# Two graph layers on one core: all matmuls of the attention layer as pairs of 64 rows, with another order of the steps

## The chip, the cores and the metric

The kernel runs on one core of a Trainium2 chip, in one launch. The metric is the time of one execution on the device, in microseconds. A core has TensorE (PE: matrix products, with PEld for its weight loads), VectorE (DVE), ScalarE (ACT), GpSimd (POOL) and SyncE (SP), which issues the DMAs here. Each engine runs its own queue in order and waits on semaphores.

## What is computed

The input `x` is 32 batches of 512 x 512, `adj` a sparse weighted 512 x 512 graph.

```python
def layer0(x, adj, weight, bias):
    y = jnp.einsum('nm,bmd->bnd', adj, x)
    out = jnp.einsum('bnd,do->bno', y, weight) + bias
    return layernorm(x + out)

def layer1(x, w_qkv, w_proj, b_proj, ln_gamma, ln_beta, attn_mask):   # 8 heads of 64
    q, k, v = (x @ w_qkv) split in heads
    attn = softmax(where(attn_mask == 0, -inf, q k^T / 8))
    o = (attn v) @ w_proj + b_proj
    ln = layernorm(o) * ln_gamma + ln_beta
    return layernorm(x + o + ln)
```

All in float32. The kernel keeps that accuracy with three products: each operand is split into a part rounded to the reduced float32 format (`_hi`) and the rest (`_lo`), and hi x hi, hi x lo and lo x hi are summed in a PSUM bank. So each product leaves PSUM in two operations: ScalarE copies it rounded (`_hi`), VectorE subtracts that from the bank (`_lo`).

## The kernel before

The first stage does layer 0 batch by batch and stores its result, normalised and turned, in DRAM (lines up to 531). The change does not touch it. The second stage does layer 1. Its unit is a step: `k` counts 16 of them in a batch, 4 pairs of heads by 4 tiles of 128 query rows. Four steps with one pair of heads are a group, and the place of a step in it is its part, 0 to 3. For each step the work is:

- `scores` (line 778): q k^T for 2 heads, 128 x 512 each. A head has 64 rows, so the two heads lie in the two halves of the array and go to two banks; six matmuls, which are three pairs. Step `k` uses one of two pairs of score banks, and TensorE issues the scores for two steps together in every second step, two and three steps ahead.
- `masked_max` (1032): VectorE adds the mask and finds the row maximum; `exponent` (932): ScalarE; `inverse` (1038): VectorE; `normalise` (708, 711): GpSimd multiplies by the inverse of the sum.
- `turn` (790): TensorE transposes the probabilities in 16 pieces of 64 rows; `pt_hi_part` (939) and `pt_lo_part` (1045) take them out of the banks.
- Once in a group, in part 3, `attend_v` (824) multiplies by v on all 128 rows: 16 matmuls into two banks, which `ot_halves` (957, 959), `ot_sum` (1063), `ot_hi_part` (965) and `ot_lo_part` (1067) take away.

Between the transposes of two steps TensorE does fill from other parts of the work, 48 matmuls of 128 rows in each group: v (`v_matmuls`, 857) in group 0, the projection of the batch before (`project`, 875) in group 1, q and k of the next batch (`qk_matmuls`, 841) in groups 2 and 3. `FILL = [20, 12, 16, 0]` spreads them over the parts. Fill and `attend_v` share the banks `g_bank`. The first batch has no projection to fill group 1, the last no next batch for groups 2 and 3. The rows of the projection are finished by VectorE, ScalarE and GpSimd at steps in the tables `O_STEP`, `Z_STEP` and `S_STEP`. `ready_to_turn` holds the waits for the probabilities and for `pt_lo` of the step before; it stands ahead of the last fill matmul. The order is written out by hand in each engine's `batch`; the loop runs over batches 1 to 30.

Of the kernel before, what the change touches and what calls it, by code (L numbers as in the profile page):

```python
# [24 lines left out]
ALU = mybir.AluOpType  # L25
# [6 lines left out]
def graph_layers(nc, x, adj, w0, b0, wqkv, wproj, bproj, gamma, beta, out):  # L32
# [19 lines left out]
    with ExitStack() as whole:  # L52
# [483 lines left out]
        with ExitStack() as second:  # L536
# [31 lines left out]
            s_bank, t_bank, g_bank = (psum[0:2], psum[2:4]), psum[4:6], psum[6:8]  # L568
            o_bank = g_bank
# [9 lines left out]
            def turned(i):  # L579
                return t_bank[i][:].rearrange("p (a m n) -> p a m n", a=2, m=T)  # L580

            def turned_into(rows, k, i):
                first = k % T * P + i * HEAD
                return rows[:, :, :, first:first + HEAD]
# [53 lines left out]
            BEFORE = [sum(FILL[:n]) for n in range(T)]  # L638
            assert sum(FILL) == 48
            assert S_STEP[-1] + 2 < STEPS  # L640
# [9 lines left out]
            def row_at(k, steps):  # L650

                return steps.index(k) if k in steps else None

            def output_at(b, k, j):

                if j == 1 and k == 5:
                    return None
                if k % T == j or (j == 1 and k == 7):  # L660
                    return (b - 1, PAIRS - 1) if k < T else (b, k // T - 1)
                return None
# [39 lines left out]
            def _(pool):  # L702
# [24 lines left out]
                def scale_and_add(b, n):  # L727
                    pool.wait_ge(z_made, b * 4 + (n - 3))
                    pool.tensor_tensor(t[:], t[:], gamma_row[:], ALU.mult).then_inc(gamma_done, 1)  # L729
                    pool.wait_ge(u_loaded, b * 64 + 16 * (n - 3))  # L730
                    pool.tensor_tensor(o[:, n, :], o[:, n, :], ub[:], ALU.add).then_inc(ub_added, 1)

                def add_z(b, n):
                    pool.wait_ge(gamma_done, b * 4 + (n - 3))
                    pool.wait_ge(ub_added, b * 4 + (n - 3))
                    pool.tensor_tensor(o[:, n, :], o[:, n, :], t[:], ALU.add).then_inc(u_added, 1)

                def batch(b, last_part=True, more=True):
                    for k in range(STEPS):
                        if last_part and row_at(k - 1, S_STEP) is not None:  # L740
                            power(b, row_at(k - 1, S_STEP), 1)
                        if k + 1 < STEPS or more:
                            normalise(b, k + 1)
                        if last_part and row_at(k - 1, Z_STEP) is not None:
                            add_z(b, row_at(k - 1, Z_STEP))
                        if last_part and row_at(k, Z_STEP) is not None:
                            scale_and_add(b, row_at(k, Z_STEP))
                        if last_part and row_at(k, O_STEP) is not None:
                            power(b, row_at(k, O_STEP), 0)
# [3 lines left out]
                with pool.Fori(1, B - 1, 1) as b:  # L753
                    batch(b)
                batch(B - 1, more=False)
                for i in range(T + 3):
# [8 lines left out]
            def _(pe):  # L765
                def scores(b, k):
# [5 lines left out]
                    for a in range(2):  # L772
                        if not (isinstance(b, int) and b * STEPS + k < 2):
                            pe.wait_ge(max_found, b * 32 + (2 * k + a - 3))
                    for i, (l, r) in enumerate(parts):
                        for a in range(2):
                            h = slice(a * HEAD, (a + 1) * HEAD)
                            last = pe.matmul(s_bank[k % 2][a][:], l[h, pair, n * P:(n + 1) * P], r[h, pair, :],  # L778
                                             start=i == 0, stop=i == 2)
                            if i == 2:  # L780
                                last.then_inc(scores_made, 1)

                def turn(k):

                    for a in range(2):
                        for m in range(T):
                            for i in range(2):
                                h = slice(i * HEAD, (i + 1) * HEAD)
# [3 lines left out]
                    last.then_inc(probs_turned, 2)  # L792

                def ready_to_turn(b, k):
                    if not (isinstance(b, int) and b * STEPS + k == 0):
                        pe.wait_ge(ptlo_made, b * 32 + 2 * k)
                    pe.wait_ge(probs_made, b * 32 + (2 * k + 2))

                def attend_v(b, p, last_part, more):
                    for a in range(2):  # L800
                        if a == 0:
                            pe.wait_ge(pthi_made, b * 32 + (8 * p + 8))

                        if p == 0:
                            if a == 0:
                                pe.wait_ge(vlo_made, b * 4 + 4)
                        elif p == 1 and last_part:
                            pe.wait_ge(o_made, b * 4 + (a - 1))
                        elif p >= 2 and more:
                            pe.wait_ge(qklo_made, b * 8 + (4 * (p - 2) + a + 11))  # L810
                        else:
                            pe.wait_ge(ot_summed, b * 8 + (2 * p + a - 1))

                        for part in (pt_hi, pt_lo):
                            if part is pt_lo and a == 0:
                                pe.wait_ge(ptlo_made, b * 32 + (8 * p + 8))
                            for m in range(T):
# [380 lines left out]
```

## Time and profile before

| | us |
|---|---|
| median of 3 runs | 3634.25 (3633.28 to 3634.72) |
| the profiled execution, time | 3633.45 |
| the profiled execution, span from first to last instruction | 3631.6 |
| TensorE busy | 3479.7 |
| VectorE busy | 2753.8 |
| ScalarE busy | 2222.5 |
| GpSimd busy | 1858.9 |

The busy time of TensorE is from rows that overlap, with ends that are modelled: a matmul that shows 0.39 us is followed by the next after 0.23. For TensorE one reads starts, not durations. The transposes' row gives 16 of them together. Times in a timeline are from the span's start.

### The profile page before, as it was taken

The page shows a single profiled execution, that of the slowest core. Times are in us where ns is not written, and L with a number is a line of the kernel's source. Part 1 is how long each engine was busy: PE and PEld are TensorE (multiplying, and loading weights), DVE is VectorE, ACT ScalarE, POOL GpSimd, SP SyncE. Part 2 cuts the span into 40 slices and gives each one's busy share as a digit, 9 for nine tenths or more (in the row PEclk, how much of TensorE's full clock was granted, in tenths as well). Part 3 has the DMA queues.
Part 4 walks back from the last instruction along what each step waited for, and adds up shares of the span by engine and source line. Part 5 has one row for each costly group of instructions (what it writes and reads, how often), then busy time and mean ns, then how long its engine had stood idle before and what let it go on. Part 6 is the DMA issues. An engine that isn't in the chain of part 4 may idle for free.

```text
span 3631.6 us, 72945 instructions
## 1 busy us (share of the span) xinstructions
PE 3479.7 (96%) x23568; PEld 2652.1 (73%) x23568; DVE 2753.8 (76%) x6557; ACT 2222.5 (61%) x4629; POOL 1858.9 (51%) x2559
## 2 busy tenths in 40 slices
PE   8999999999999999999999999999999999999996
PEld 6888888876777777777777777777777777777774
DVE  7666666646787777778777787877777777777777
ACT  4444444436666666666666666666666666666664
POOL 4555555533555555555555555555555554555555
PEclk9999999999999999999999999999999999999997
DMA  6555555541111111111111111111111111111110
GB/s 192 176 179 178 177 183 176 182 142 34 59 49 46 46 49 46 46 47 48 46 46 46 49 46 46 46 46 46 46 47 58 48 46 46 46 46 46 51 53 33
DMA packets 344962, 276.26 MB, mean 76 GB/s; under 512 B 13664, under 2 KB 275808, under 8 KB 344928
## 3 DMA queue, kind: packets, MB, share of 16 engines
q1 hardware_dynamic: 344928, 275.83, 24.7%
q8 instruction: 18, 0.29, 0.0%
q14 instruction: 16, 0.13, 0.0%
HBM read 141.56 MB, written 134.22 MB: 76 GB/s over the span
## 4 chain that ended last, share of the span: by engine, by line
PE 38%; issue 22%; DVE 15%; ACT 15%; POOL 8%; ACTq 0%; SPq 0%; POOLq 0%; DMA 0%; DVEq 0%
PE bank L841 9%; PE bank L824 8%; PE bank L857 7%; PE bank L875 7%; ACT probs L932 6%; DVE pt_lo L1045 6%; PE bank L790 5%; POOL xb L302 4%; ACT pt_hi L939 4%; POOL ub L296 3%; PE bank L778 3%; DVE probs L1032 2%; ACT ot_hi L965 2%; ACT k_hi L943 1%; DVE o_stats L1071 1%
## 5 line engine op out<-in xcount | busy, mean ns | idle before, releaser
L932 ACT ACTIVATE probs<-probs,bias_row 128x512 f32<-128x512 f32 x1024 | 729.0, 713 | 482.0 <-DVE bias_row L1032 482.0
L1045 DVE TENSOR_TENSOR pt_lo<-bank,pt_hi 128x512 fp32r<-128x512 f32 x1024 | 655.4, 681 | 97.8 <-ACT pt_hi L939 93.7
L711 POOL TENSOR_SCALAR probs<-probs,inv_sums 128x480 f32<-128x480 f32 (+1 forms) x1024 | 685.0, 682 | 0.0
L1032 DVE CUSTOM_DVE_ANT_0 probs<-bank,mask_bias 128x512 f32<-128x512 f32 x1024 | 660.7, 682 | 0.0
L939 ACT ACTIVATE pt_hi<-bank 128x512 fp32r<-128x512 f32 x1024 | 553.3, 593 | 142.9 <-PE bank L790 136.6
L708 POOL TENSOR_TENSOR probs<-probs,inv_sums 128x32 f32<-128x32 f32 x512 | 122.2, 239 | 984.8 <-DVE inv_sums L1038 981.0
L841 PE MATMUL bank<-x_hi,w_hi 128*128 128x512 f32 x1024 | 415.3, 406 | 58.5 <-DVE ot L1063 27.9
L790 PEld LDWEIGHTS bank<-ident,probs 64*128 64x128 f32 x8192 | 296.3, 139 | 204.5 <-issue 177.3
L841 PE MATMUL bank<-x_hi,w_lo 128*128 128x512 f32 x1024 | 414.3, 405 | 0.0
L841 PE MATMUL bank<-x_lo,w_hi 128*128 128x512 f32 x1024 | 401.2, 392 | 0.0
L790 PE MATMUL bank<-ident,probs 64*128 64x64 f32 x8192 | 366.6, 230 | 25.1 <-POOL probs L711 25.1
L824 PE MATMUL bank<-pt_hi,v 128*128 128x512 f32 x1024 | 292.0, 407 | 35.1 <-ACT pt_hi L939 35.1
L717 POOL TENSOR_TENSOR o_rstd<-o_var_eps,half_neg 128x1 f32<-128x1 f32 x256 | 141.8, 554 | 298.5 <-DVE o_var_eps L1076 297.8
L391 ACT ACTIVATE u<-res,shift,rstd 128x512 f32<-128x512 f32 x128 | 104.6, 817 | 306.8 <-DVE shift L474 306.8
L824 PE MATMUL bank<-pt_lo,v 128*128 128x512 f32 x1024 | 290.1, 405 | 0.0
L1063 DVE TENSOR_TENSOR ot<-bank,ot 64x512 f32<-64x512 f32 x256 | 176.3, 689 | 147.1 <-ACT ot L957 126.2
L841 PEld LDWEIGHTS bank<-x_hi,w_hi 128*128 128x128 f32 x1024 | 193.0, 189 | 125.1 <-DVE k_lo L1051 45.5
L824 PEld LDWEIGHTS bank<-pt_hi,v 128*128 128x128 f32 x1024 | 183.6, 189 | 120.9 <-DVE k_lo L1051 51.2
L307 POOL TENSOR_TENSOR rstd<-var_eps,half_neg 128x1 f32<-128x1 f32 x128 | 95.8, 748 | 339.8 <-DVE var_eps L469 339.8
L841 PEld LDWEIGHTS bank<-x_hi,w_lo 128*128 128x128 f32 x1024 | 192.7, 188 | 64.4 <-issue 22.3
L824 PEld LDWEIGHTS bank<-pt_lo,v 128*128 128x128 f32 x1024 | 183.0, 188 | 68.9 <-DVE pt_lo L1045 36.1
L729 POOL TENSOR_TENSOR t<-t,gamma_row 128x512 f32<-128x512 f32 x124 | 160.6, 1296 | 131.2 <-ACT t L971 131.2
(90 smaller groups left out, 7842.4 us busy)
## 6 DMA issues: line engine op xcount, KB each, us to landing
x_in<-in_x_dram SPq DMA_DIRECT2D x32, 1024.0 KB, 5.3
u_beta_rows<-ub SPq DMA_DIRECT2D x32, 1024.0 KB, 4.4
ut_hi<-ut_hi_sb SPq DMA_DIRECT2D x128, 256.0 KB, 4.2
ut_lo<-ut_lo_sb SPq DMA_DIRECT2D x128, 256.0 KB, 3.8
x_hi<-ut_hi SPq DMA_DIRECT2D x128, 256.0 KB, 4.3
x_lo<-ut_lo SPq DMA_DIRECT2D x128, 256.0 KB, 4.6
out_dram<-o SPq DMA_DIRECT2D x128, 256.0 KB, 3.3
ub_row<-u_beta_rows SPq DMA_DIRECT2D x124, 256.0 KB, 2.7
```

Of the source, the lines that this page charges most:

```text
L711: pool.tensor_scalar(probs[:, k % 2, a, cols], probs[:, k % 2, a, cols], inv_sums[:, k % 4, a:a + 1], 0.0, ALU.mult, ALU.add)\
L729: pool.tensor_tensor(t[:], t[:], gamma_row[:], ALU.mult).then_inc(gamma_done, 1)
L790: last = pe.transpose(t_bank[i][:, cols], probs[h, k % 2, a, m * P:(m + 1) * P], ident[h, h])
L824: last = pe.matmul(o_bank[a][:], w, part[:, a, m, :], start=part is pt_hi and m == 0, stop=part is pt_lo and m == T - 1)
L841: last = pe.matmul(g_bank[i % 2][:], a[:, w, m, pair * P:(pair + 1) * P], c[:, m, :], start=g % 12 == 0, stop=g % 12 == 11)
L857: last = pe.matmul(g_bank[n % 2][:], a[:, m, n * P:(n + 1) * P], c[:, 2, m, :], start=g % 12 == 0, stop=g % 12 == 11)
L875: last = pe.matmul(g_bank[n % 2][:], a[:, p, n * P:(n + 1) * P], c[:, 3, p, :], start=g % 12 == 0, stop=g % 12 == 11)
L932: act.activation(probs[:, k % 2, a, :], probs[:, k % 2, a, :], ACT.Exp, bias=bias_row[:, k % 4, a:a + 1], scale=-1.0, accum_out=sums[:, k ...
L939: act.activation(turned_into(pt_hi, k, i), turned(i), ACT.Copy).then_inc(pthi_made, 1)
L1032: dve.tensor_tensor_reduce(probs[:, k % 2, a, :], s_bank[k % 2][a][:], mask_bias[:, k % T, :], -SCALE, 3.0e38, ALU.add, ALU.min, bias_row[ ...
L1045: dve.tensor_tensor(turned_into(pt_lo, k, a), turned(a), f32(turned_into(pt_hi, k, a)), ALU.subtract).then_inc(ptlo_made, 1)
L1063: dve.tensor_tensor(ot[h, :], o_bank[a][h, :], ot[h, :], ALU.add).then_inc(ot_summed, 1)
```

## The change

- **Pairs.** Fill and `attend_v` are split over the 64 upper (`TOP`) and 64 lower (`BOTTOM`) rows of the array. `half_pair` issues a matmul in each half, into two different banks. Twelve pairs (a run) do the upper rows of one product and the lower rows of the other; in the second run the banks are swapped, behind a wait for the first (`v_half`, `proj_half`, `qk_half`, `pv_half`). Two products are thus ready together after 24 pairs. The transposes and scores stay as they are.
- **Banks.** One pair of banks for scores in place of two; `attend_v` has a pair of its own, `o_bank`; fill has these and two more.
- **Scores** are issued one step at a time, three steps ahead. They wait until the maximum of the step before has been taken (`max_found`).
- **VectorE** does the reciprocal and the maximum first in a step, and then the lower halves; ahead of the reciprocal it waits for this step's transposes.
- **Outputs.** `attend_v` is cut in four parts: scores stand between the first two, two pairs of fill ahead of the fourth.
- **Fill** of a group begins in part 2 of the group before (`EARLY = (4, 6, 2)`), the rest lies in parts 0 to 2.
- The row work moves to later steps, with new `O_STEP`, `Z_STEP` and `S_STEP`; the last row of a batch ends in the batch after.

```diff
-            s_bank, t_bank, g_bank = (psum[0:2], psum[2:4]), psum[4:6], psum[6:8]
-            o_bank = g_bank
+            s_bank, t_bank, o_bank = psum[0:2], psum[2:4], psum[4:6]
+            g_bank = psum[6:8] + o_bank
...
-            O_STEP = [4, 5, 6, 7]
-            Z_STEP = [5, 7, 9, 11]
-            S_STEP = [8, 11, 12, 13]
-            FILL = [20, 12, 16, 0]
+            O_STEP = [5, 7, 7, 11]
+            Z_STEP = [7, 9, 11, 13]
+            S_STEP = [9, 11, 13, 15]
+            EARLY = (4, 6, 2)
+            FILL = ((8, 4), (12, 4), (8, 0))
...
+                    if not (isinstance(b, int) and b * STEPS + k == 0):
+                        pe.wait_ge(max_found, b * 32 + 2 * k)
...
+                def half_pair(banks, left, right, run, first, end):
+                    top = pe.matmul(banks[run][:], left[run][TOP], right[run][TOP], start=run == 0 and first,
+                                    stop=run == 1 and end)
+                    bottom = pe.matmul(banks[1 - run][:], left[1 - run][BOTTOM], right[1 - run][BOTTOM],
+                                       start=run == 0 and first, stop=run == 1 and end)
+                    return top, bottom
...
+                    def step(k, group, part):
+                        filled = group == 0 or (last_part if group == 1 else more)
+                        begin, (front, back) = BEFORE[part], FILL[part]
+                        turn(k)
+                        fill(group, begin, front)
+                        if k + 3 < STEPS or more:
+                            scores(b, k + 3)
+                        if part == 2:
+                            group, begin, front, back = group + 1, 0, 0, EARLY[0]
+                            filled = group < PAIRS and (last_part if group == 1 else more) or group == PAIRS and more
+                        if filled:
+                            fill(group, begin + front, back - 1)
+                        ready_to_turn(b, k + 1)
+                        if filled:
+                            fill(group, begin + front + back - 1, 1)
+                    def last_step(k, group):
+                        turn(k)
+                        fill(group + 1, EARLY[0], EARLY[1])
...
+                        attend_v(b, group, pt_hi, 0)
+                        if k + 3 < STEPS or more:
+                            scores(b, k + 3)
+                        attend_v(b, group, pt_hi, 1)
+                        attend_v(b, group, pt_lo, 1)
+                        fill(group + 1, EARLY[0] + EARLY[1], EARLY[2])
+                        attend_v(b, group, pt_lo, 0)
...
-                def inverse(b, k):
+                def inverse(b, k, before_max=False):
                     dve.wait_ge(exp_made, b * 32 + (2 * k + 2))
+                    if before_max:
+                        scores_at(b, k + 1)
+                        dve.wait_ge(probs_turned, b * 32 + 2 * k)
                     dve.reciprocal(inv_sums[:, k % 4, :], sums[:, k % 4, :]).then_inc(inv_made, 1)
...
                 def batch(b, last_part=True, more=True):
                     for k in range(STEPS):
...
+                        if k + 1 < STEPS or more:
+                            inverse(b, k + 1, before_max=ahead)
+                        if ahead:
+                            masked_max(b, k + 2, waited=True)
+                        pt_lo_part(b, k)
                         if output_at(b, k, 0) and (last_part or k >= T):
                             ot_sum(*output_at(b, k, 0))
```

The order of instructions shows two places. On TensorE, part 3 of group 3 in the loop before (L778 scores, L824 `attend_v`):

```order
L778 MATMUL bank<-k_lo,q_hi 128x512 x2
L778 MATMUL bank<-k_hi,q_lo 128x512 x2
...
L824 MATMUL bank<-pt_hi,v 128x512 [waits qklo_made]
L824 MATMUL bank<-pt_hi,v 128x512 x3
L824 MATMUL bank<-pt_lo,v 128x512 [waits ptlo_made]
L824 MATMUL bank<-pt_lo,v 128x512 x3
...
L824 MATMUL bank<-pt_hi,v 128x512 [waits qklo_made]
L824 MATMUL bank<-pt_hi,v 128x512 x3
L824 MATMUL bank<-pt_lo,v 128x512 x3
```

and in the changed kernel (L840 `attend_v`, L800 scores, L849 and L851 the two pieces of a fill pair):

```order
L840 MATMUL bank<-pt_hi,v 128x512 [waits pthi_made,qklo_made]
L840 MATMUL bank<-pt_hi,v 128x512 x7
L800 MATMUL bank<-k_hi,q_hi 128x512 [waits max_found]
...
L800 MATMUL bank<-k_lo,q_hi 128x512 x2
...
L840 MATMUL bank<-pt_hi,v 128x512 [waits pv_half]
L840 MATMUL bank<-pt_hi,v 128x512 x7
L840 MATMUL bank<-pt_lo,v 128x512 [waits ptlo_made]
L840 MATMUL bank<-pt_lo,v 128x512 x7
L849 MATMUL bank<-w_lo,x_hi 128x512
L851 MATMUL bank<-w_lo,x_hi 128x512
...
L840 MATMUL bank<-pt_lo,v 128x512 [waits pv_half]
L840 MATMUL bank<-pt_lo,v 128x512 x5
```

The sixteen full matmuls have become sixteen pairs in four parts, the scores and two pairs of fill have moved between these, and each part after the first waits for something of its own.

On VectorE, step 8 in the loop before, from the sums of the output to the maximum (L1038 is the reciprocal, L1045 `pt_lo`, L1032 the maximum; bank numbers shown):

```order
L1063 TENSOR_TENSOR ot<-bank6,ot 64x512 [waits ot_half]
...
L1063 TENSOR_TENSOR ot<-bank7,ot 64x512 [waits ot_half]
L1038 RECIPROCAL inv_sums<-sums 128x2 [waits exp_made]
...
L1045 TENSOR_TENSOR pt_lo<-bank4,pt_hi 128x8x64 [waits pthi_made]
...
L1045 TENSOR_TENSOR pt_lo<-bank5,pt_hi 128x8x64 [waits scores_made]
L1032 ISA probs,bias_row<-bank0,mask_bias 128x512
...
L1032 ISA probs,bias_row<-bank1,mask_bias 128x512
```

and in the changed kernel (L1122 the reciprocal, L1113 the maximum, L1130 `pt_lo`, L1148 the output's sums):

```order
L1122 RECIPROCAL inv_sums<-sums 128x2 [waits probs_turned,scores_made]
L1113 ISA probs,bias_row<-bank0,mask_bias 128x512
...
L1113 ISA probs,bias_row<-bank1,mask_bias 128x512
...
L1130 TENSOR_TENSOR pt_lo<-bank2,pt_hi 128x8x64 [waits pthi_made]
L1130 TENSOR_TENSOR pt_lo<-bank3,pt_hi 128x8x64 [waits pthi_made]
...
L1148 TENSOR_TENSOR ot<-bank4,ot 64x512 [waits ot_half]
...
L1148 TENSOR_TENSOR ot<-bank5,ot 64x512 [waits ot_half]
```

The reciprocal and the maximum have moved from behind to ahead, behind a wait for the transposes; the maximum reads banks 0 and 1 in every step, and the output comes out of banks 4 and 5.

## Rows read from the trace of the kernel before

**Rows 1.** The page, part 1: busy time (us), share of the span, instructions.
```profile
PE 3479.7 (96%) x23568; PEld 2652.1 (73%) x23568; DVE 2753.8 (76%) x6557; ACT 2222.5 (61%) x4629; POOL 1858.9 (51%) x2559
```

**Rows 2.** Windows: width, then busy time by engine, clock, DMA, in the steady loop.
```profile
860.00:2600.00 1740.00, 1685.82 (x12077) 1256.77 (x12077) 1379.07 (x3401) 1175.72 (x2537) 888.76 (x1343) 1.00 0.16 47
```

**Rows 3.** Timeline of TensorE, first `attend_v` rows of two successive batches (start, duration, engine, line, idle).
```profile
1914.24 1.19 PE L824 MATMUL bank<-pt_hi,v 128*128 128x512 f32 x4 [0.33 <-ACT pt_hi L939]
...
2001.94 1.19 PE L824 MATMUL bank<-pt_hi,v 128*128 128x512 f32 x4 [0.33 <-ACT pt_hi L939]
```

**Rows 4.** Timeline of TensorE: transposes, scores and fill in one step.
```profile
1111.87 0.71 PE L790 MATMUL bank<-ident,probs 64*128 64x64 f32 x16
1112.39 0.47 PE L778 MATMUL bank<-k_hi,q_hi 64*128 64x512 f32 x2
1112.70 0.40 PE L778 MATMUL bank<-k_lo,q_hi 64*128 64x512 f32 x2
...
1113.63 0.40 PE L778 MATMUL bank<-k_hi,q_lo 64*128 64x512 f32 x2
1113.96 0.50 PE L841 MATMUL bank<-x_hi,w_lo 128*128 128x512 f32 x1
1114.30 0.40 PE L841 MATMUL bank<-x_hi,w_hi 128*128 128x512 f32 x1
```

**Rows 5.** Timeline of TensorE: a fill, transposes, and a fill after transposes.
```profile
3543.05 0.39 PE L875 MATMUL bank<-w_lo,ot_hi 128*128 128x512 f32 x1
...
3545.77 0.39 PE L875 MATMUL bank<-w_lo,ot_hi 128*128 128x512 f32 x1
3546.09 0.71 PE L790 MATMUL bank<-ident,probs 64*128 64x64 f32 x16
...
3551.13 0.71 PE L790 MATMUL bank<-ident,probs 64*128 64x64 f32 x16
3551.77 0.50 PE L875 MATMUL bank<-w_hi,ot_lo 128*128 128x512 f32 x1
3552.10 0.39 PE L875 MATMUL bank<-w_hi,ot_hi 128*128 128x512 f32 x1
```

**Rows 6.** Timeline of TensorE: last scores before `attend_v`, and its start.
```profile
1101.15 0.40 PE L778 MATMUL bank<-k_hi,q_lo 64*128 64x512 f32 x2
1101.48 1.20 PE L824 MATMUL bank<-pt_hi,v 128*128 128x512 f32 x4
1102.52 1.19 PE L824 MATMUL bank<-pt_lo,v 128*128 128x512 f32 x4
1103.54 1.08 PE L824 MATMUL bank<-pt_hi,v 128*128 128x512 f32 x4
```

**Rows 7.** Waits from 900 to 3400 us: who waited for whom, us, times, longest.
```profile
PE bank L824 <- ACT pt_hi L939: 31.3, 85, 0.5
PE bank L841 <- DVE ot L1063: 26.9, 29, 1.0
PE bank L841 <- DVE k_lo L1051: 19.0, 28, 0.7
```

**Rows 8.** Timeline of VectorE: pieces of steps in the loop.
```profile
2004.19 0.69 DVE L1071 BATCH_NORM_STATS2 o_stats<-o 128x6 f32<-128x512 f32 x1
...
2005.97 1.41 DVE L1063 TENSOR_TENSOR ot<-bank,ot 64x512 f32<-64x512 f32 x2 [0.62 <-ACT ot L957]
...
2018.17 0.15 DVE L1038 RECIPROCAL inv_sums<-sums 128x2 f32<-128x2 f32 x1
2018.24 1.27 DVE L1045 TENSOR_TENSOR pt_lo<-bank,pt_hi 128x512 fp32r<-128x512 f32 x2
2019.42 0.20 DVE L1081 TENSOR_SCALAR o_shift<-o_mean_var,o_rstd 128x1 f32<-128x1 f32 x1
2019.55 0.68 DVE L1032 CUSTOM_DVE_ANT_0 probs<-bank,mask_bias 128x512 f32<-128x512 f32 x1
```

**Rows 9.** Timeline of ScalarE: upper halves behind the transposes.
```profile
1112.62 1.09 ACT L939 ACTIVATE pt_hi<-bank 128x512 fp32r<-128x512 f32 x2 [0.68 <-PE bank L790]
```

More of the change, by code:

```diff
@@ new lines, in half_pair, with qk_matmuls @@
+                def half_pair(banks, left, right, run, first, end):
[4 more added lines that the diff above has]
+                    return top, bottom
+                def qk_matmuls(b, first, count):
+                    begin = isinstance(b, int) and b == 0
@@ L840, in qk_matmuls @@
                         a, c = ((w_hi, xt_hi), (w_hi, xt_lo), (w_lo, xt_hi))[s]
-                        last = pe.matmul(g_bank[i % 2][:], a[:, w, m, pair * P:(pair + 1) * P], c[:, m, :],
-                                         start=g % 12 == 0, stop=g % 12 == 11)
+                        pair = i // 2
+                        pieces = half_pair([g_bank[i % 4], g_bank[i % 4 + 1]],
+                                           [a[:, w, m, pair * P:(pair + 1) * P] for w in range(2)], [c[:, m, :]] * 2,
+                                           run, g % 12 == 0, g % 12 == 11)
@@ L874, in project @@
                         a, c = ((ot_hi, w_hi), (ot_hi, w_lo), (ot_lo, w_hi))[s]
-                        last = pe.matmul(g_bank[n % 2][:], a[:, p, n * P:(n + 1) * P], c[:, 3, p, :],
-                                         start=g % 12 == 0, stop=g % 12 == 11)
+                        pieces = half_pair([g_bank[n], g_bank[n + 1]],
+                                           [a[:, p, (n + w) * P:(n + w + 1) * P] for w in range(2)],
+                                           [c[:, 3, p, :]] * 2, run, g % 12 == 0, g % 12 == 11)
@@ L877, in project, with fill @@
                         if g % 12 == 11:
-                            last.then_inc(proj_done, 1)
+                            for piece in pieces:
+                                piece.then_inc(proj_done if run else proj_half, 1)
                 def batch(b, last_part=True, more=True):
-                    for k in range(STEPS):
-                        group, part = divmod(k, T)
+                    def fill(group, first, count):
+                        if group == 0:
+                            v_matmuls(b, first, count)
+                        elif group == 1 and last_part:
+                            project(b, first, count)
+                        elif 2 <= group < PAIRS and more:
+                            qk_matmuls(b + 1, 48 * (group - 2) + first, count)
+                        elif group == PAIRS and more:
+                            v_matmuls(b + 1, first, count)
@@ L907, in _ @@
+                    for group in range(PAIRS):
+                        for part in range(T - 1):
+                            step(T * group + part, group, part)
+                        last_step(T * group + T - 1, group)
                 last_turn(pe, 0)
-                qk_matmuls(0, 0, 12, begin=True)
-                qk_matmuls(0, 12, 12, begin=True)
+                qk_matmuls(0, 0, 12)
+                qk_matmuls(0, 12, 12)
                 last_turn(pe, 1)
-                qk_matmuls(0, 24, 12, begin=True)
+                qk_matmuls(0, 24, 12)
@@ L1008, in _ @@
                 exponent(0, 0)
+                qk_hi_part(0, 2)
                 qk_hi_part(0, 3)
```

356 lines of the change are left out of this document (183 added, 173 removed).

## The prediction

> **What bounds the kernel now.** I read the page's part 1 first: TensorE is busy in 96% of the span, VectorE in 76% [rows 1]. TensorE's rows overlap, so this says only that it is rarely idle. The windows of the steady loop say the same at full clock (1.00, the 2.4 GHz level): of 1740 us, TensorE 1686, VectorE 1379, ScalarE 1176, GpSimd 889 [rows 2]. The timeline gives the period. The same `attend_v` starts at 1914.24 and at 2001.94, so one batch takes 87.70 us [rows 3], and thirty batches (1 to 30) run in this form.
>
> Then I asked what those 87.70 us are made of. All per batch, from starts of rows:
> - 48 pairs of half-row matmuls for the scores. Pairs start at 1112.70 and, four pairs later, at 1113.63: 0.2325 us each [rows 4], 11.2 us.
> - 192 fill matmuls and 64 of `attend_v`, on all 128 rows. From 3543.05 to 3545.77 there are twelve starts: 0.227 each [rows 5]; 256 make 58.1.
> - 16 groups of 16 transposes, on 64 rows. To the scores that follow, 1111.87 to 1112.39, 0.52 [rows 4]: 8.3.
> - Changes between 64-row and 128-row work. Transposes to fill take 0.64 (3551.13 to 3551.77), 0.12 more than to scores, and the second fill matmul then comes 0.33 after the first, 0.10 more than usual. Fill to transposes takes 0.32 (3545.77 to 3546.09), 0.09 more [rows 5]. Scores to fill take 0.33 (1113.63 to 1113.96), 0.10 more, and the first fill gap is 0.34, 0.11 more [rows 4]. Scores to `attend_v` is 0.33 as well, and its first four matmuls take 1.04 where four take 0.91, 0.13 more [rows 6]. The first pair of scores after transposes has 0.31, 0.08 more than 0.2325, without any change of form [rows 4]; so a small part stays whatever is done.
>
> A group of four steps has two plain ones (0.31 each), one with scores and fill (0.08 + 0.10 + 0.11 + 0.09 = 0.38), one with scores and `attend_v` (0.08 + 0.10 + 0.13 + 0.09 = 0.40). That is 1.40 a group, 5.6 a batch. The sum is 11.2 + 58.1 + 8.3 + 5.6 = 83.2. The missing 4.5 us are waits: on ScalarE's upper halves before `attend_v`, and on VectorE's sums and lower halves before the first fill of a group, 77.2 us of idle over 28.5 batches or 2.7 each [rows 7], and the rest in waits too short to show as idle, such as 1101.48 to 1103.54, two fours that take 2.06 where 1.82 is due [rows 6].
>
> **What the change does to TensorE.** Every full-row matmul becomes two on 64 rows, one in each half of the array, into two banks. 256 pairs replace 256 matmuls, and no change of form is left in the loop. No row shows a pair of fill, but the scores are such pairs, with the same 128 columns of weights and 512 columns of data, so I take 0.2325. Its ends are 0.227 (as one full matmul) and, if the halves ran one after the other, 0.454; I stay at the scores' row because it has the same shape.
> - 304 pairs at 0.2325: 70.7. Transposes: 8.3. The first pair behind each of 16 groups of transposes, 0.08: 1.3. Together 80.3.
> - Pair to transposes: no row without a change of form; between 0 and 0.09 each. I take 0.05, 0.8 a batch (ends 0 and 1.4).
> - New waits of TensorE on itself. The two runs of a half swap banks, so the second run waits for the first (`v_half` and its like). The fills' swap falls at matmul 12, behind transposes, and at 36, behind scores. In `attend_v` three pairs of scores (0.70) or two of fill (0.47) stand between. A matmul shows 0.39 from start to end [rows 5], so a wait asked 0.70 behind the last issue is free, one behind 0.47 nearly so.
>
> **What it does to waits.** Let a step's transposes start at 0. ScalarE's upper half starts at 0.75 (transposes at 1111.87, ScalarE at 1112.62, after standing idle), and two take 1.09 [rows 4, 9], so they end at 1.85. `attend_v` now comes after six pairs of fill, at 0.52 + 0.08 + 1.40 = 2.0, so its wait goes. The first fills of a group write other banks than `attend_v` and begin two steps early; the waits on `ot` and `k_lo` [rows 7] go with it. Late next is the maximum: with one pair of score banks, `scores(k+3)` must wait for the maximum of k+2. VectorE's queue at a step is now reciprocal, two maxima, two lower halves, then the rest. From [rows 8]: reciprocal 0.07, lower halves 1.18 (2018.24 to 2019.42), each maximum 0.61 to the next start (an estimate: the row's 0.68 less 0.08, by which the reciprocal's row overlaps the next one). If it too starts at 0.75, the maxima are done at 2.1, and with 0.1 for the signal TensorE is free at 2.2. It comes there at 0.60 + 8 x 0.2325 = 2.46 in parts 0 and 2, at 3.4 in part 1, and at 2.9 in part 3. The slack is 0.25 in the first two. Lower halves end at 3.3, and are asked for at 3.86 at the earliest (before the last of 15 pairs).
>
> So all hangs on VectorE being back when the transposes end. Steps of TensorE: 15 pairs in parts 0 and 2, 4.1 us; 19 in part 1, 5.0; 27 in part 3, 6.9. VectorE's list, from 0.75: part 0 to 3.3, then two `ot` sums at 1.41 [rows 8], 4.7 of 4.85 allowed. Part 1 to 3.3, two halves or `add_bproj` 1.2, and in steps 5, 9 and 13 statistics. These are 0.61 for the row at 2004.19 and about 0.5 for what hangs on it, so 5.7 to 5.8 of 5.75. Part 2: 4.5, with `ot_lo` in group 0 5.0, of 4.85. Part 3: at most two statistics and `ot_lo`, 6.4 of 7.65. It just fits: lags of 0.0 to 0.15 against a slack of 0.25, and part 3 gives all back. I put 0.04 on each of twelve narrow places, 0.5 a batch; the ends are 0 and 1.7 (0.14 each, as the gap of 0.24 in [rows 6] over its two changes and one wait suggests).
>
> A batch then takes 80.3 + 0.8 + 0.5 = 81.6, with ends at 80.3 and 83.4. That is 6.1 less than 87.7; over 30 batches 183 us. Batches 0 and 31 have the change of form in part of their groups, about 3 each. The steps there without fill are paced by VectorE and GpSimd in both orders, and I take no change. The last projection now delivers rows 0 and 1 together after 24 pairs, not after 12 matmuls, 2.8 us later (12 x 0.2325) on the path to the end. Net 3 us. ScalarE and GpSimd have two thirds and half of their time busy [rows 2], and the row work given later steps lands in these holes.
>
> The profiled execution took 3633.45, 0.8 under the median of 3634.25; its span is 3631.6. So 3633.45 - 183 - 3 = 3447. With the ends of the batch, 30 x 4.3 and 30 x 7.4 less, that is 3501 and 3408.
>
> **Two rules of the Trainium skill.** The changes of form cost 0.12, 0.10 and 0.09 above [rows 5]. The Trainium skill, TensorEngine Tiling (Array Packing), section Key Properties, says that changing the tiling mode drains the engine, while tiles of one mode run independently. By it all of the 5.6 but the 1.3 goes, as in my sum. Against the change speaks the Trainium skill, TensorE: Matmul & The Clock Gate, section The cost: per-tile semaphore tail: increments by every tile's matmul follow one another at 26.3 ns. Both pieces of a pair now increment at the end of each run, 24 increments more a batch, an estimate of 0.6 us or 19 in all, and 3466. The scores already do it: both pieces of their third pair increment, and the four gaps from 1112.70 to 1113.63, in which that falls, still average 0.2325 [rows 4]; so the sum has no term for it.
>
> **Rivals.**
> A. As summed: 3447, range 3408 to 3501. Chance 0.64.
> B. VectorE sets the pace. For: 1379 of 1740 us are busy now, in a loop that gets 7% shorter, with lists that fit to 0.1, and it must stand still until the transposes are done. If each of parts 0 to 2 runs 0.3 longer than I count, 0.9 less the slack of 0.25 is lost in a group, 2.6 a batch, 78 in all: about 3525. Against: part 3 has over a microsecond of air. Chance 0.13.
> C. Long streams of pairs go slower than six in a row, say 0.245, halfway to the point at which the gain is gone: 256 x 0.0125 = 3.2 a batch, 96 in all: 3543. Chance 0.12.
> D. Slower than before. A pair loads two sets of weights. If these pass one path, a pair takes as long as two loads, and the change loses from 0.2325 + 6.1 / 256 = 0.256 us a pair. With the two halves wholly in series (0.454) a batch takes 57 us more and the kernel some 5150; at 0.28, 12.2 a batch, 365 in all on 3447, or 3812. The pitch of the scores speaks against. Chance 0.05, with 3812 as its time.
> E. It doesn't do what it says: the gaps belong to what follows transposes or a wait, not to a change of form, and stay. Then only the waits go: 80.3 + (5.6 - 1.3) + 1.3 = 85.9, 1.8 less a batch, 54 in all: 3577. Against it is the 0.52 to scores beside 0.64 to fill. Chance 0.06.
>
> **Numbers.** A is likeliest: 3447. A and B and most of C make the range, 3405 to 3535. About 0.2% (7 us) is what a measurement can tell from no change. A, B, C and nearly all of E lie below that: faster 0.94; 0.01 within; slower 0.05.
>
> **What would show it.** The period of `attend_v` falls to 81 to 82 us. Starts of fill pairs are 0.23 apart through a run, and 0.31 only behind transposes. Fill to transposes takes under 0.28. Idle of TensorE before fill and before `attend_v` is gone, and any wait that has taken its place stands before the scores, on the maximum. VectorE is busy over 84% of the loop. The forecast fails if pairs lie over 0.245 apart, or if TensorE waits more than 0.1 a step for VectorE.

## The result, and the profile after

| | before | changed |
|---|---|---|
| median of 4 runs, us | 3634.48 (3633.28 to 3634.74) | 3515.89 (3512.27 to 3519.12) |
| profiled execution, us | 3633.45 | 3518.51 |
| period of a batch in the loop, us | 87.70 | 83.87 (mean of 30) |

The ratio is 0.9674, 95% interval 0.9657 to 0.9691: faster by 119 us, where 187 had been forecast. The time lies in the range (3405 to 3535), 69 us above the point, and above the 3408 to 3501 that rival A, the sum itself, had for its ends.

The page of the changed kernel, its busy times and its instruction queue (packets, MB, share); beside it that queue's line of before:

```profile
PE 3358.9 (96%) x31760; PEld 2823.5 (80%) x31760; DVE 2684.0 (76%) x6557; ACT 2211.1 (63%) x4629; POOL 1830.8 (52%) x2559
...
q8 instruction: 285, 4.67, 0.5%
```

```profile
q8 instruction: 18, 0.29, 0.0%
```

TensorE's share, 96%, is as in [rows 1]; the instruction queue is what differs, 4.67 MB for 0.29. The steady loop, as [rows 2] has it (width, busy by engine, clock, DMA):

```profile
860.00:2600.00 1740.00, 1678.79 (x17916) 1421.34 (x17916) 1392.04 (x3544) 1218.80 (x2647) 903.07 (x1395) 0.99 0.18 51
```

The clock is 0.99 where it was 1.00. The first `attend_v` of five successive groups (timeline, compare [rows 3]):

```profile
1847.71 1.20 PE L840 MATMUL bank<-pt_hi,v 64*128 64x512 f32 x8
...
1867.76 1.19 PE L840 MATMUL bank<-pt_hi,v 64*128 64x512 f32 x8
...
1887.79 1.19 PE L840 MATMUL bank<-pt_hi,v 64*128 64x512 f32 x8
...
1911.86 1.19 PE L840 MATMUL bank<-pt_hi,v 64*128 64x512 f32 x8
...
1931.93 1.20 PE L840 MATMUL bank<-pt_hi,v 64*128 64x512 f32 x8
```

Three of the four distances are 20.03 to 20.07 us, 80.2 in a batch of four such, close to the bare sum of the prediction, 80.3. The one from 1887.79 to 1911.86 is 24.07. Transposes, and the fill behind them (compare [rows 4, 5]):

```profile
1900.77 0.39 PE L849 MATMUL bank<-w_hi,x_lo 64*128 64x512 f32 x1
...
1900.99 0.68 PE L816 MATMUL bank<-ident,probs 64*128 64x64 f32 x16
1901.46 0.47 PE L849 MATMUL bank<-w_hi,x_hi 64*128 64x512 f32 x1
...
1901.77 0.39 PE L849 MATMUL bank<-w_lo,x_hi 64*128 64x512 f32 x1
...
1902.00 0.39 PE L849 MATMUL bank<-w_hi,x_lo 64*128 64x512 f32 x1
```

Pairs stand 0.23 apart, fill to transposes is 0.22 and no longer 0.32, transposes to fill 0.47 and no longer 0.64, and the first gap is 0.31. The waits of [rows 7] are gone from TensorE's list, and one that no row of before had is there (900 to 3400 us; total, times, longest):

```profile
PE bank L816 <- issue: 79.6, 29, 3.1
```

"Issue" means that the profile shows nothing that TensorE waited for. There is one such stop in each batch but the first of the loop: 29, as many as the loop of 30 batches jumps back. The stretch around one of them, at the place where TensorE's loop jumps back to its first instruction:

```profile
1891.78 1.10 PE L840 MATMUL bank<-pt_lo,v 64*128 64x512 f32 x8
1895.39 0.71 PE L816 MATMUL bank<-ident,probs 64*128 64x64 f32 x16 [2.50 <-issue]
1895.88 0.49 PE L849 MATMUL bank<-w_hi,x_hi 64*128 64x512 f32 x1
...
1896.19 0.60 PE L849 MATMUL bank<-w_lo,x_hi 64*128 64x512 f32 x1
...
1896.60 0.62 PE L849 MATMUL bank<-w_hi,x_lo 64*128 64x512 f32 x1
...
1898.73 0.62 PE L849 MATMUL bank<-w_lo,x_hi 64*128 64x512 f32 x1
...
1899.15 0.64 PE L800 MATMUL bank<-k_hi,q_hi 64*128 64x512 f32 x2
```

The last eight pieces of `attend_v` start at 1891.78, so the transposes were due at 1892.71. They start at 1895.39, 2.7 us late, while nothing holds them but "issue". Then pairs stand 0.42 to 0.43 apart in place of 0.23. The windows (columns as in [rows 2]) show that the clock is lower there. From 1892 to 1896 VectorE, ScalarE and GpSimd do nothing either, and behind that TensorE's granted clock is 0.57 for four microseconds, mostly its lower level of 1.2 GHz.

```profile
1892.00:1896.00 4.00, 1.50 (x26) 1.03 (x24) 0.00 (x0) 0.00 (x0) 0.00 (x0) 1.00 0.03 8
1896.00:1900.00 4.00, 4.00 (x26) 3.66 (x24) 3.83 (x9) 3.79 (x8) 2.07 (x4) 0.57 0.00 0
1900.00:1904.00 4.00, 4.00 (x49) 3.69 (x48) 2.42 (x9) 2.29 (x6) 1.56 (x3) 1.00 0.02 4
```

So this jump costs twice: the stop, and the half clock after it. Not every jump does. Behind 11 of the 29 stops the clock stays at 1.00, as here (timeline, then window):

```profile
1812.53 0.71 PE L816 MATMUL bank<-ident,probs 64*128 64x64 f32 x16 [3.02 <-issue]
```

```profile
1812.00:1816.00 4.00, 3.47 (x42) 3.22 (x44) 2.72 (x8) 2.64 (x5) 2.08 (x4) 1.00 0.02 4
```

The group with the jump takes 22.88 us on average in these 11 and 24.32 in the other 18, against 20.07 for a group without: 2.8 us for the stop each time, and 1.4 more where the clock fell. Together that is 3.7 a jump and 107 us. The stops before were about as long in both cases (2.7 and 2.8 us), and what decides between them is not shown.

### The profile page after: what moved, and what is told of

The parts are those of the page before. It is cut to its first block, busy times and chain, and to the rows that moved or that the text cites. A ratio compares the mean times of both kernels' runs of the same rounds, so it can differ in the third digit from the quotient of the medians.

```text
span 3516.7 us, 89066 instructions
## 1 busy us (share of the span) xinstructions
PE 3358.9 (96%) x31760; PEld 2823.5 (80%) x31760; DVE 2684.0 (76%) x6557; ACT 2211.1 (63%) x4629; POOL 1830.8 (52%) x2559
## 3 DMA queue, kind: packets, MB, share of 16 engines
q8 instruction: 285, 4.67, 0.5%
## 4 chain that ended last, share of the span: by engine, by line
PE 64%; issue 17%; DVE 10%; POOL 8%; ACT 0%; SPq 0%; POOLq 0%; DMA 0%; DVEq 0%
PE bank L849 31%; PE bank L840 14%; PE bank L800 8%; PE bank L816 6%; POOL xb L302 4%; PE bank L851 4%; DVE ot L1148 4%; POOL ub L296 4%; DVE pt_lo L1130 3%; DVE probs L1113 2%; DVE inv_sums L1122 0%; DVE bias_row L1113 0%; PE bank L339 0%; POOL rstd L307 0%; DMA x_lo<-ut_lo 0%
## 5 line engine op out<-in xcount | busy, mean ns | idle before, releaser
L1113 DVE CUSTOM_DVE_ANT_0 probs<-bank,mask_bias 128x512 f32<-128x512 f32 x1024 | 661.2, 683 | 9.9 <-PE bank L800 5.7
L1130 DVE TENSOR_TENSOR pt_lo<-bank,pt_hi 128x512 fp32r<-128x512 f32 x1024 | 656.7, 683 | 2.0 <-ACT pt_hi L1019 2.0
L816 PEld LDWEIGHTS bank<-ident,probs 64*128 64x128 f32 x8192 | 344.2, 140 | 155.7 <-issue 95.8
L1122 DVE RECIPROCAL inv_sums<-sums 128x2 f32<-128x2 f32 x512 | 83.4, 163 | 458.4 <-PE bank L816 446.3
L816 PE MATMUL bank<-ident,probs 64*128 64x64 f32 x8192 | 344.8, 223 | 87.2 <-issue 79.6
L849 PE MATMUL bank<-x_hi,w_hi 64*128 64x512 f32 x1024 | 413.5, 404 | 13.1 <-DMA x_lo<-ut_lo 5.5
L851 PE MATMUL bank<-x_hi,w_hi 64*128 64x512 f32 x1024 | 413.3, 404 | 0.0
L849 PE MATMUL bank<-x_lo,w_hi 64*128 64x512 f32 x1024 | 409.9, 400 | 0.0
L851 PE MATMUL bank<-x_lo,w_hi 64*128 64x512 f32 x1024 | 409.9, 400 | 0.0
L849 PE MATMUL bank<-x_hi,w_lo 64*128 64x512 f32 x1024 | 398.4, 389 | 0.0
L851 PE MATMUL bank<-x_hi,w_lo 64*128 64x512 f32 x1024 | 398.3, 389 | 0.0
L840 PE MATMUL bank<-pt_hi,v 64*128 64x512 f32 x2048 | 297.3, 405 | 5.2 <-ACT pt_hi L1019 5.1
L840 PE MATMUL bank<-pt_lo,v 64*128 64x512 f32 x2048 | 279.6, 388 | 0.3
L840 PEld LDWEIGHTS bank<-pt_hi,v 64*128 64x128 f32 x2048 | 208.8, 187 | 50.1 <-issue 34.0
L849 PEld LDWEIGHTS bank<-x_hi,w_hi 64*128 64x128 f32 x1024 | 189.9, 185 | 54.6 <-DVE ot L1148 14.0
```

Source lines behind the costliest of these rows:

```text
L816: last = pe.transpose(t_bank[i][:, cols], probs[h, k % 2, a, m * P:(m + 1) * P], ident[h, h])
L840: last = pe.matmul(o_bank[a][:], w, part[h, a, m, :], start=first and m == 0, stop=end and m == T - 1)
L849: top = pe.matmul(banks[run][:], left[run][TOP], right[run][TOP], start=run == 0 and first, stop=run == 1 and end)
L851: bottom = pe.matmul(banks[1 - run][:], left[1 - run][BOTTOM], right[1 - run][BOTTOM], start=run == 0 and first, stop=run == 1 and end)
L1113: dve.tensor_tensor_reduce(probs[:, k % 2, a, :], s_bank[a][:], mask_bias[:, k % T, :], -SCALE, 3.0e38, ALU.add, ALU.min, bias_row[:, k % ...
L1130: dve.tensor_tensor(turned_into(pt_lo, k, i), turned(i), f32(turned_into(pt_hi, k, i)), ALU.subtract).then_inc(ptlo_made, 1)
```

## The experiments

All ratios are to the kernel before on the same chip; differences between two runs can go across chips, on which the kernel before took 3633.7 to 3635.7 us. "Straight" means that TensorE's batches 1 to 30 stand one after the other in the program and not in a loop.

**1. No jump in the changed kernel.**

```diff
-                with pe.Fori(1, B - 1, 1) as b:
+                for b in range(1, B - 1):
                     batch(b)
```

> The changed kernel, with TensorE's loop over batches 1 to 30 written out as straight code; all else the same. In the changed kernel TensorE stands still once in a batch, 2.5 to 3.1 us ahead of the first transposes of the loop's body, with no other engine named, and then runs at half clock to the end of the first fill; the group with this place takes 24.07 us against 20.05 for the others, so 4.0 us a batch. Theory 1 (the jump back in a body too large to be kept): straight code has no jump, and 30 x 4.0 = 120 us go: about 3396 us, with every group at 20.05 and no idle marked issue. Theory 2 (the number of instructions per us is more than can be fetched, and the stall is only where it shows): the same instructions are fetched, so 3516 us, with stalls spread over the batch. Theory 3 (something of the batch's start, a wait on another engine): 3516 us, the stall at the same place.

Measured 3408.57 us (3405.27 to 3409.82), ratio 0.9375 (0.9359 to 0.9391). No idle marked issue is left. A batch takes 80.13:

```profile
1904.53 1.19 PE L840 MATMUL bank<-pt_hi,v 64*128 64x512 f32 x8
...
1984.66 1.19 PE L840 MATMUL bank<-pt_hi,v 64*128 64x512 f32 x8
```

107 us went. That is 13 less than expected: the jumps back are 29 and not 30, and a group with a jump is 3.7 us longer on average of all 29, where the 4.0 came from one of them. Theories 2 and 3 fall. The straight program moves 3.64 MB through the instruction queue, so instructions still move; it just holds nothing up. This is the fastest kernel of the study.

**2. Two batches in the body.**

```diff
-                with pe.Fori(1, B - 1, 1) as b:
+                with pe.Fori(1, B - 1, 2) as b:
                     batch(b)
+                    batch(b + 1)
```

> The changed kernel, with two batches in the body of TensorE's loop, so 15 jumps back in place of 30. Theory 1: the cost is one per jump, half of 120 us goes: about 3456 us, every second batch boundary free of the stall. Theory 2: 3516 us. Theory 3: 3516 us, the stall in every batch.

Measured 3469.70 us (3464.28 to 3473.81), ratio 0.9539 (0.9523 to 0.9555). 61 us above straight code, and 14 stops in the trace (a loop of 15 rounds jumps back 14 times): 4.4 a jump, where 30 rounds had 3.7. The cost goes with the jumps, though not in strict proportion: here the clock fell behind 11 of 14 stops, there behind 18 of 29.

**3. The same edit in the kernel before**, which has neither pairs nor the new order.

> The kernel before, in its old order and with its full-row matmuls, but with two batches in the body of TensorE's loop. Its body has 608 matmuls a batch, the changed kernel's 864; two batches make 1216, more than the changed kernel's body. Theory 1: it gets the stall that it never had, in each of 15 jumps, about 4 us: 3634 + 60 = 3694 us, and the instruction queue moves some MB in place of 0.3. Theories 2 and 3: no change, 3634 us, since the work and the rate of instructions are the same.

Measured 3711.98 us (3710.68 to 3716.20), ratio 1.0211 (1.0194 to 1.0229): slower by 76 us, 5.4 for each of 14 jumps. In the trace the group with the jump takes 26.70 us on average, 5.4 more than the 21.32 of the same group without it, and the clock falls behind every one. The size of the body alone has made the stall in the old kernel (timeline of TensorE at a jump, two stops, and the fill's first gap at 0.51 behind them where 0.33 is usual):

```profile
1970.93 0.71 PE L790 MATMUL bank<-ident,probs 64*128 64x64 f32 x16 [1.14 <-issue]
1973.94 0.71 PE L857 MATMUL bank<-w_hi,x_hi 128*128 128x512 f32 x1 [2.29 <-issue]
1974.45 0.63 PE L857 MATMUL bank<-w_lo,x_hi 128*128 128x512 f32 x1
```

**4. No jump in the kernel before.** The edit of 1.

> The kernel before with TensorE's loop over batches 1 to 30 written out as straight code. It shows no idle marked issue at its jump. If a jump in a body of 608 matmuls is free (theory 1), nothing changes: 3635 us, within 5. If every jump costs something, even a kept one, up to 30 x 1 us less: 3605. With this kernel the gain of the pairs and the new order is measured without jumps on either side.

Measured 3636.90 us (3635.02 to 3637.92), ratio 1.0005 (0.9995 to 1.0014). A jump in the small body costs nothing that shows.

**5. How large a body may be.** `one_full` is a full matmul in place of a pair, used for q and k, then for the projection as well; the loop is kept.

```diff
+                def one_full(banks, left, right, run, first, end):
+                    return (pe.matmul(banks[run][:], left[run], right[run], start=first, stop=end),)
...
-                        pieces = half_pair([g_bank[i % 4], g_bank[i % 4 + 1]],
+                        pieces = one_full([g_bank[i % 4], g_bank[i % 4 + 1]],
```

> The changed kernel, its loop over 30 batches kept, with the fill for q and k as full matmuls on 128 rows (v, projection and attend_v stay pairs). The loop's body has 768 matmuls, against 608 in the kernel before, which shows no stall at the jump, and 864 in the changed kernel, which does. Bounds the size from which the jump costs. Groups 2 and 3 get the changes of form that the same order with full matmuls everywhere showed (22.50 against 20.05, less what attend_v has of it), so about 2.2 us more each, 4.4 a batch: 3516 + 132 = 3648 us if the stall stays, 3528 us if it goes. Theory 1 only says that one of the two comes, with idle marked issue in the first and none in the second.

> As the one with q and k full, and the projection too as full matmuls: 720 matmuls in the body. Another 2.2 us a batch for group 1: about 3714 us with the stall, 3594 us without. The idle marked issue tells which. If the size of the body counts, a kernel with the stall here must have it at 768 too, and one without it at 768 must have none here.

With 768 matmuls in the body: 3763.40 us, ratio 1.0356 (1.0326 to 1.0386), with two stops at each jump:

```profile
1901.77 1.01 PE L816 MATMUL bank<-ident,probs 64*128 64x64 f32 x14 [2.53 <-issue]
1904.77 0.37 PE L816 MATMUL bank<-ident,probs 64*128 64x64 f32 x2 [1.99 <-issue]
```

With 720 matmuls: 3640.01 us, ratio 1.0017 (1.0005 to 1.0028), no idle marked issue, and little in the instruction queue:

```profile
q8 instruction: 20, 0.33, 0.0%
```

The limit in this program lies between 720 and 768 matmuls (each with its weight load). Both times were above what I expected, by some 46 and 115 us, and the starts of `attend_v` in the traces take this apart. With 768, the four groups take 20.05 (on the way into the loop, where there is no jump), 20.6, 22.6 and 22.0, or 85.3 a batch where I had 84.5 (80.1 and 4.4). The group with the jump takes 26.98 on average of 29, 6.9 more than 20.05, where I had 4.0: the two stops together are 4.8, and the clock falls behind each. 30 x (85.3 - 80.13) + 29 x 6.9 is 355 us above straight code, which gives 3764. With 720, the groups take 20.55, 22.57, 22.58 and 22.00, or 87.7 where I had 86.7. So the cost of a jump is not one number: the smaller body of 768 pays more than that of 864. Why it stops twice stays open.

**6. The new order without the pairs.** Fill and `attend_v` as full matmuls everywhere, loop kept.

```diff
-                    return top, bottom
+                    return (pe.matmul(banks[run][:], left[run], right[run], start=first, stop=end),)
...
-                        for a, h in ((run, TOP), (1 - run, BOTTOM)):
-                            w = v[h, m, 2 * p + a, :, :].rearrange("p s d -> p (s d)")
+                        w = v[:, m, 2 * p + run, :, :].rearrange("p s d -> p (s d)")
```

> The changed kernel's order, banks, and steps, but each pair of 64-row matmuls in fill and attend_v is one matmul on 128 rows (the first run does one product, the second the other), so that the changes of form are back and the loop's body has 608 matmuls again. The output is the same product sums. My sum: 58.1 for the matmuls, 11.2 for scores, 8.3 for transposes, 5.6 to 6 for changes of form (attend_v now has one more, around the scores, and fill stands on both sides of the scores in parts 0, 1), which is 83.2 plus some 1.2 for the two to three more changes in a group, so 84.4 a batch against 87.7: 3634 - 30 x 3.3 = 3535 us. Theory 1: no stall at the jump, as before, 3535. Theories 2: also none. Theory 3 (the stall belongs to the new order at the batch's start): 4.0 more a batch, 3655 us. If the changes of form cost nothing and only the waits counted, it would be 79.5 a batch and 3388 us.

Measured 3714.71 us (3712.60 to 3717.47), ratio 1.0217 (1.0200 to 1.0234), slower than before, and missed by 180 us: I had counted two or three more changes of form in a group. In fact the scores now stand apart from the transposes in every step: eight stretches of 64 rows in a group where before had four. TensorE's timeline, one group (1902.63 to 1925.13 is 22.50 us, against 20.05):

```profile
1902.63 1.09 PE L839 MATMUL bank<-pt_hi,v 128*128 128x512 f32 x4
...
1910.30 0.39 PE L848 MATMUL bank<-w_lo,ot_hi 128*128 128x512 f32 x1
1910.62 0.50 PE L800 MATMUL bank<-k_hi,q_hi 64*128 64x512 f32 x2
1910.95 0.40 PE L800 MATMUL bank<-k_lo,q_hi 64*128 64x512 f32 x2
...
1911.19 0.40 PE L800 MATMUL bank<-k_hi,q_lo 64*128 64x512 f32 x2
1911.51 0.50 PE L848 MATMUL bank<-w_hi,ot_lo 128*128 128x512 f32 x1
1911.85 0.40 PE L848 MATMUL bank<-w_hi,ot_hi 128*128 128x512 f32 x1
...
1925.13 1.09 PE L839 MATMUL bank<-pt_hi,v 128*128 128x512 f32 x4
```

The scores between two fills cost 0.09 on the way in (1910.30 to 1910.62 is 0.32), 0.10 in their first gap, and 0.09 and 0.11 on the way out, 0.39 in all. No wait of TensorE's matmuls is left in the list. So the order alone loses 80 us although it removes the waits. On this order, with straight code for the pairs and a loop that shows no stop for the full matmuls, the pairs are worth 3714.71 - 3408.57 = 306 us. The pairs in the old order were not run.

**7. The maximum behind the lower halves**, in straight code.

```diff
+                        pt_lo_part(b, k)
                         if ahead:
                             masked_max(b, k + 2, waited=True)
-                        pt_lo_part(b, k)
```

> The changed kernel with straight code, but VectorE does the two lower halves (pt_lo) first and then the maxima, as before the change. Theory of the prediction: scores(k+3) waits for the maximum of k+2, which would be done at 0.75 + 0.08 + 1.2 + 1.2, with some waiting on ScalarE's second half, at 3.5 to 3.9 after the transposes begin, in place of 2.1. TensorE comes to it at 2.46 in parts 0 and 2, 3.4 in part 1, 2.9 in part 3, so it loses 1.0 to 1.5 twice, 0.1 to 0.5, and 0.6 to 1.0 in a group: 2.7 to 4.5 us, 11 to 18 a batch, 3410 + 350 to 560: 3760 to 3970 us, slower than the kernel before. Rival (VectorE's total work counts, not its order): 3410 us.

Measured 4036.36 us, ratio 1.1104 (1.1085 to 1.1122), 628 above straight code, 4.9 a group against the 2.7 to 4.5 expected, so above the upper end of 3970. TensorE's wait is where it was named, at the scores, 336 times in 2100 us, which is 4.0 a group; the other 0.9 I did not look for:

```profile
PE bank L800 <- DVE bias_row L1113: 339.8, 336, 1.5
```

The rival falls: VectorE does the same work in both.

**8. `attend_v` in one piece**, straight code: the four parts, then the two pairs of fill, then the scores.

> The changed kernel with straight code, but the four parts of attend_v follow each other directly, with the two pairs of fill and the scores behind them. The same instructions in another order. Theory: two parts in each group then wait for the end of the part just before (swap of banks); a matmul shows 0.39 from start to end, its follower is due at 0.23, and the signal and the next weight load come on top, so 0.2 to 0.5 us for each wait, 8 in a batch, 256 in all: 50 to 130 us, 3460 to 3540 us. Rival (such a wait costs nothing, the queue runs on): 3410 us, and the cutting in four parts brings nothing.

Measured 3500.09 us, ratio 0.9630 (0.9614 to 0.9646), 91.5 above straight code: 0.36 for each of 256 waits. Timeline:

```profile
2006.64 2.46 PE L840 MATMUL bank<-pt_hi,v 64*128 64x512 f32 x16
2008.94 2.36 PE L840 MATMUL bank<-pt_lo,v 64*128 64x512 f32 x16
2011.13 0.39 PE L849 MATMUL bank<-x_lo,w_hi 64*128 64x512 f32 x1
```

Each row is two parts, eight pairs, for which 1.86 is due; they take 2.30 and 2.19, 0.44 and 0.33 more. These are waits of TensorE for its own last matmul, and no row shows them as idle.

**9. No fill between transposes and `attend_v`**, straight code.

```diff
-            EARLY = (4, 6, 2)
+            EARLY = (10, 0, 2)
```

> The changed kernel with straight code and EARLY = (10, 0, 2): the six pairs of fill between the transposes of part 3 and attend_v stand at the end of part 2 instead. Theory: attend_v then comes 0.6 after its transposes begin, while ScalarE's upper halves are done at 1.85, so TensorE waits about 1.3 us in each group, 5.2 a batch, 128 groups: 3410 + 166 = 3576 us. VectorE's slack in part 2 grows by 1.4, which brings nothing if VectorE is not what counts. Rival (VectorE's lag in part 2 is the hidden price, and the shift frees it): less than half of that, under 3490 us.

Measured 3579.83 us, ratio 0.9847 (0.9830 to 0.9863), 171 above straight code where 166 was expected:

```profile
PE bank L840 <- ACT pt_hi L1019: 127.2, 98, 1.3
```

## Why the prediction was right, and what failed in it

- **The range was hit in part by luck.** The way and the mechanism were right: the changes of form and the waits before `attend_v` went. But 119 us were gained where 187 had been forecast, and 3515.89 lies outside 3408 to 3501, the ends of the sum. It is inside the range because that was carried up to 3535 for rivals B and C, and neither came about. What filled the room is a cost that nobody had named.
- **The pitch of a pair, 0.2325.** Right: 0.23 through whole fills, 0.231 on average of the 18 pairs from 1914.49 to 1918.64 in straight code. It rested on bursts of six. Rivals C and D fall.
- **Changes of form.** Right that they go (E falls). Experiment 6 gives their price in another order. The Trainium skill, TensorEngine Tiling (Array Packing), section Key Properties, has the engine drained by a change of tiling mode. The trace agrees as far as it goes: with no change left, fill to transposes takes 0.22 for 0.32, and transposes to fill 0.47 for 0.64.
- **Pair to transposes, 0.8 a batch, and narrow places, 0.5.** Both mis-sized: 0.22 from pair to transposes is no gap at all, and a batch without jump takes 80.13 where 81.6 was forecast. Over 30 batches that is 44 us less than I counted, and it hid part of the miss. That 80.13 is so near the bare 80.3 is itself luck. The pieces are shorter than their rows of before: 0.46 from transposes to the next pair in 225 of 337 steps read from 900 to 3200 us, where 0.52 was put, and 0.231 a pair. Against that stands a wait.
- **VectorE just fits (B).** Right for the maximum, which is what B was about. In straight code its step 9 runs with no gap above 0.1, the last statistics ending as the next reciprocal starts, and TensorE does not wait for the maximum:

```profile
1914.26 0.15 DVE L1122 RECIPROCAL inv_sums<-sums 128x2 f32<-128x2 f32 x1
1914.44 0.69 DVE L1113 CUSTOM_DVE_ANT_0 probs<-bank,mask_bias 128x512 f32<-128x512 f32 x1
...
1915.67 1.29 DVE L1130 TENSOR_TENSOR pt_lo<-bank,pt_hi 128x512 fp32r<-128x512 f32 x2
1916.87 0.21 DVE L1166 TENSOR_SCALAR o_shift<-o_mean_var,o_rstd 128x1 f32<-128x1 f32 x1
1916.99 0.68 DVE L1136 TENSOR_TENSOR q_lo<-bank,q_hi 128x512 fp32r<-128x512 f32 x1
...
1918.19 0.69 DVE L1156 BATCH_NORM_STATS2 o_stats<-o 128x6 f32<-128x512 f32 x1
1918.98 0.18 DVE L1159 BATCH_NORM_AGGREGATE o_mean_var<-o_stats 128x2 f32<-128x6 f32 x1
1919.19 0.15 DVE L1161 TENSOR_SCALAR o_var_eps<-o_mean_var 128x1 f32<-128x1 f32 x1
1919.43 0.17 DVE L1122 RECIPROCAL inv_sums<-sums 128x2 f32<-128x2 f32 x1
```

  Reciprocal at 1914.26 to reciprocal at 1919.43 is 5.17 against TensorE's 5.0, near the list (5.7 to 5.8 of 5.75, both counted from 0.75). Experiment 7 shows that the order in the queue carries this.
- **The waits on `ot` do not all go.** The prediction struck them, since the first fills of a group write other banks. But from its 25th pair on, in part 1, the fill takes `attend_v`'s two banks (`o_bank`), and must wait until VectorE's sums have read them. In straight code (timelines of TensorE, of its weight loads and of VectorE):

```profile
1913.40 0.71 PE L816 MATMUL bank<-ident,probs 64*128 64x64 f32 x16
```

```profile
1914.15 0.18 PEld L849 LDWEIGHTS bank<-x_hi,w_hi 64*128 64x128 f32 x1 [0.17 <-DVE ot L1148]
```

```profile
1912.69 1.40 DVE L1148 TENSOR_TENSOR ot<-bank,ot 64x512 f32<-64x512 f32 x2
```

  The sums end at 1914.09, and the pair that was due at 1913.86 starts at 1914.15. It is so once in every group: 112 steps take 0.66 to 0.77 from transposes to fill where the others take 0.46. That is 0.27 each, 1.1 a batch and some 32 us in 30 batches, too short to show as idle of the matmuls. So VectorE holds TensorE up after all, at a place that the prediction had not on its list.
- **New waits of TensorE on itself.** Right where something stands between; experiment 8 gives 0.36 us where nothing does.
- **What covers the upper halves.** Right, by experiment 9 to within 5 us.
- **The semaphore increments.** To have no term for them was right: the gap behind the last pair of a run, 1916.82 to 1917.05 in straight code, is 0.23 as any other. The number of increments was wrong, without effect: the program has 48 more a batch and not 24, 16 each at the fill, at `attend_v` and at the transposes.
- **The step that failed: the sum took TensorE's instructions as free.** The change makes 864 matmuls of 608 in the loop's body; the prediction counted what they cost in the array and not how they come to the engine, and no rival named it. Shown in its place: 107 us for 29 jumps (experiment 1), 61 for 14 (2), made in the old kernel by size alone (3), absent in the small body (4), with its limit between 720 and 768 (5). The Trainium skill says it in Runtime: NRT & Kernel Launch, section Instruction fetch mechanics: instructions are fetched ahead in order, and a taken branch whose target is no longer held stops the engine until it is fetched. The runs agree, with 2.7 us for the stop. What fills these 2.7 us is not shown in full: of the instruction queue one packet of 0.02 MB moves between 1892.5 and 1893.0, early in the stop, and none from there to 1895.5. The estimate by these numbers, 3447 - 44 + 107, is 3510, against 3515.89 measured.
- **The signs that were named.** Starts 0.23 apart, fill to transposes under 0.28 and no idle before fill and `attend_v` came true. The period of 81 to 82 did not (83.87, and 80.13 without jumps), nor did VectorE's 84%: it is busy for 1392 of 1740 us, 80%, and for 1458, 84%, in straight code.
- **The ends.** 30 x (87.70 - 80.13) = 227 us, and straight code is 226 under the kernel before. So the net of 3 us from first and last batch and tail is not seen; I did not take it apart.

## What to carry to other kernels

When a change adds instructions to a loop's body, count them: look at the page's instruction queue (0.29 MB before, 4.67 MB after) and at idle marked issue behind the jump, and if the idle is there, write the loop out or keep the body small. Put 64-row and 128-row matmuls in as few stretches as possible, or make all of them 64-row pairs, which cost 2% in pitch (0.231 for 0.227). A new order can look bad alone: here it loses 80 us by itself, while with the pairs it is 226 us faster than before; whether the pairs need it was not tested. Ask of every bank who read it last, not only of the one that is written first.

## What the runs showed of the hardware

- A jump in TensorE's loop cost nothing with 608 matmuls in the body and showed no stop with 720. It cost 3.7 us on average with 864, 4.4 with 1728, 5.4 with 1216 and about 6.9 with 768; the last two had two stops at each jump. With 864 the stop was 2.7 us, and behind 18 of 29 stops the granted clock fell to the 1.2 GHz level (0.57 over 4 us in the one shown), 1.4 us more.
- A second run of pairs that waited for the end of the one just before it cost 0.36 us (experiment 8).
- A stretch of three pairs of scores between fills of full matmuls cost 0.39 us beyond its own time (experiment 6).
